# Second attention's scores as twelve 32-row products in row groups instead of four 128-row products

## What is computed

```python
q = proj(hs, Wq, bq, S); k = proj(at, Wk, bk, T); v = proj(at, Wv, bv, T)   # heads of 32 columns
scores = jnp.einsum('bhsd,bhtd->bhst', q, k) / scale
scores = jnp.clip(scores, -50.0, 50.0)
attend = (attention_mask.astype(jnp.float32) > 0.5)[:, None, None, :]
scores = jnp.where(attend, scores, -10000.0)
scores = jnp.clip(scores, -50.0, 50.0)
probs = jax.nn.softmax(scores, axis=-1)
ctx = jnp.einsum('bhst,bhtd->bhsd', probs, v)
```

## Time and profile before

| | us |
|---|---|
| median of 3 runs (2567.28 to 2568.74) | 2568.36 |
| span of the profiled execution | 2568.4 |
| second attention: first clip starts | 1822.25 |
| second attention: last clip ends | 2353.85 |

### The profile page before, as it was taken

The page is one execution under the profiler, slowest core; times in us unless marked ns, Lnnn a source line. Parts: engine busy times, 40 slices in busy tenths (PEclk is TensorE's granted clock), DMA queues, the critical chain, the costliest instruction groups (busy, mean ns, idle before and its releaser), DMA issues. The chain is left out here.

```text
span 2568.4 us, 33913 instructions
## 1 busy us (share of the span) xinstructions
PE 2506.9 (98%) x13273; PEld 1626.8 (63%) x13288; DVE 1786.5 (70%) x2456; ACT 1223.6 (48%) x1853; POOL 1286.9 (50%) x340
## 2 busy tenths in 40 slices
PE   8999999999999999999998999999999999999998
PEld 8988888987545545555544787788533333335786
DVE  4554554556777767777774676664899999999873
ACT  4222313311666666666664232322688888886110
POOL 0000000000999999999993000000599999997310
PEclk9999999999999999999999999999999999999999
DMA  8677776655535345354323754443997777776300
GB/s 303 212 255 236 265 283 240 221 172 160 115 83 121 68 96 108 68 111 93 68 71 137 246 185 156 155 164 87 245 213 168 167 159 167 159 170 196 120 33 33
DMA packets 218865, 405.10 MB, mean 158 GB/s; under 512 B 18217, under 2 KB 94537, under 8 KB 218641
## 3 DMA queue, kind: packets, MB, share of 16 engines
q1 hardware_dynamic: 218704, 402.93, 56.8%
HBM read 260.63 MB, written 140.59 MB: 156 GB/s over the span
## 5 line engine op out<-in xcount | busy, mean ns | idle before, releaser
L1486 POOL TENSOR_TENSOR pooled<-pooled,probs 128x2048 f32<-128x2048 f32 x140 | 641.5, 4582 | 21.0 <-POOL pooled L1486 0.9
L1345 ACT ACTIVATE probs<-psum 128x512 f32<-128x512 f32 (+1 forms) x832 | 449.6, 600 | 333.6 <-PE psum L1231 328.4
L1372 DVE TENSOR_REDUCE win_max<-psum 128x1 f32<-128x802 f32 x480 | 454.3, 988 | 133.9 <-PE psum L1196 133.6
L2271 DVE TENSOR_SCALAR probs<-psum,bound 128x1024 f32<-128x1024 f32 (+1 forms) x416 | 499.0, 1275 | 31.5 <-POOL pooled L2303 21.3
L2246 ACT ACTIVATE probs<-probs 128x1024 f32<-128x1024 f32 (+1 forms) x416 | 437.6, 1059 | 82.5 <-DVE probs L2271 40.6
L2303 POOL TENSOR_TENSOR pooled<-pooled,probs 128x2048 f32<-128x2048 f32 x92 | 424.2, 4611 | 13.2 <-ACT probs L2246 1.0
L1231 PE MATMUL psum<-q_st,k_st 128*128 128x512 f32 (+1 forms) x832 | 318.7, 436 | 22.2 <-ACT probs L1345 15.6
L312 POOL TENSOR_TENSOR r_q<-ve_q,minus_half 128x4 f32<-128x4 f32 x8 | 9.1, 1133 | 611.3 <-DVE ve_q L256 611.3
L1196 PE MATMUL psum<-k_st,q_st 96*128 96x402 f32 x960 | 265.8, 358 | 0.9 <-DVE o_sb L1391 0.4
L1231 PEld LDWEIGHTS psum<-q_st,k_st 128*128 128x128 f32 (+1 forms) x832 | 149.4, 185 | 180.4 <-ACT probs L1345 130.6
L2214 PE MATMUL psum<-q_st,k_st 128*128 128x512 f32 (+1 forms) x832 | 251.6, 428 | 10.7 <-DVE probs L2271 9.6
(11 more groups left out here) (276 smaller groups left out, 4211.1 us busy)
## 6 DMA issues: line engine op xcount, KB each, us to landing
k_st<-k_hi SPq DMA_DIRECT2D x64, 801.0 KB, 10.6
k_st<-k_lo SPq DMA_DIRECT2D x48, 801.0 KB, 11.1
k_hi<-kt_hi SPq DMA_DIRECT2D x32, 801.0 KB
k_lo<-kt_lo SPq DMA_DIRECT2D x32, 801.0 KB
v_rows<-v_out SPq DMA_DIRECT2D x96, 256.0 KB
v_st<-v_rows SPq DMA_DIRECT2D x24, 768.0 KB
q_st<-q_hi SPq DMA_DIRECT2D x64, 256.0 KB, 8.4
w<-w_hi_d SPq DMA_DIRECT2D x64, 256.0 KB, 3.1
```

The source lines that it names most:

```text
L1345: A.activation(probs[i % NPROBS][0:rows, j, :], bank(score_banks.where["score", u, t, j])[0:rows, :], ACT.Exp, scale=1.0 / ROOT).then_inc( ...
L1372: V.tensor_reduce(win_max[:, r, j, c:c + 1], window(windows.where["max", u, i])[:, :, 0:MV], AX.XY, ALU.max).then_inc(max_done, 1)
L1486: G.tensor_tensor(pooled[u % 2][:], before[:], probs[tile(u, k) % NPROBS][:], ALU.add).then_inc(pool_added, 1)
L2271: V.tensor_scalar(probs[i % NPROBS][0:rows, half * W:half * W + W, :], window(("score", u, t, half))[0:rows], bound[0:rows, u // NG, t:t + 1],
```

## The change

Keys and queries keep their natural layout: 128 partitions for the four heads, the high and the low part side by side. A head's product now has 32 rows and lies in the head's own row group of the array (partitions 32j to 32j+31). A tile's scores are three rounds (high by high, high by low, low by high; the low-by-low product is gone), each of four 32-row products, one for each head and row group, into the head's own bank. All twelve follow the waits for both of the tile's windows, and `scored` is signalled in the third round only. Turns give way to steps: one tile's scores, then values and sums of the tile two behind. `last_sum` moves behind the values of tile 1 (step 3), the copy of the sums behind the exponentials of step 3, `copy_acc` behind the first one of step 1. The loads are two a unit for keys and two for queries in place of four and four.

```diff
-            n, NQ, NSLOT = 1, 4, 3
+            n, NQ, NSLOT, LAG = 1, 2, 3, 2
+            TERMS = ((0, 0), (0, 1), (1, 0))
-            PER_TURN, ACC_COPY, DEN_COPY, LAST_SUM = 3, (1, 0), (2, 2), 2
-            VALUES = [[-2], [-1], [0, 1], [2], [3, 4], [5], [6, 7], [8], [9, 10]]
-            TURNS, SUM_LATER = len(VALUES), TT - 3
+            ACC_COPY, DEN_COPY, LAST_SUM, SUM_LATER = (1, 0), (3, 1), 1, TT - 3
...
+                def steps():
                     for u in range(UNITS):
+                        for t in range(TT):
+                            yield u, t, divmod(tile(u, t) - LAG, TT) if tile(u, t) >= LAG else None
...
+                    def scores(u, t):
+                        s, rows = u % NSLOT, TROWS[t]
+                        ps = []
+                        for half in range(HALVES):
+                            pair = take(("score", u, t, half))
+                            windows.freed_by(clipped, score(u, t, half) + 1)
+                            ps += [pair[0:rows, w, :] for w in range(W)]
...
-                        for w in range(W):
-                            m = M.matmul(ps[0:rows, w, :], k_st[s][:, j + w, t * P:t * P + rows],
-                                         q_st[s][:, j + w, :], start=True, stop=True)
-                        m.then_inc(scored, 1)
+                        for i, (of_k, of_q) in enumerate(TERMS):
+                            for j in range(HPG):
+                                head = slice(j * DH, (j + 1) * DH)
+                                m = M.matmul(ps[j], k_st[s][head, of_k, t * P:t * P + rows], q_st[s][head, of_q, :],
+                                             start=i == 0, stop=i == len(TERMS) - 1)
+                                if i == len(TERMS) - 1 and j % W == W - 1:
+                                    m.then_inc(scored, 1)
+
+                    for u, t, behind in steps():
+                        scores(u, t)
+                        if behind:
+                            values(*behind)
+                            if behind != (UNITS - 1, SUM_LATER):
+                                sums(*behind)
+                            if behind[0] and behind[1] == LAST_SUM:
+                                last_sum(behind[0] - 1)
...
                     def load_kq(u):
                         s = u % NSLOT
+                        for h in range(NQ):
                             if u > 1:
+                                load(k_st[s][:, h, :], (k_hi, k_lo)[h][n][u], kq_landed[s])
+                            load(q_st[s][:, h, :], (q_hi, q_lo)[h][n][u], kq_landed[s])
```

More of the change, by code:

```diff
@@ L2048, in sp_program @@
                     Y.wait_ge(hidden_ps, B * FT)
[L2049 to L2054, removed]
+                    for h in range(2):
+                        load(early_k[0][:, h, :], (k_hi, k_lo)[h][1][0], early_landed)
+                        load(x_hi[:, h, :], (q_hi, q_lo)[h][1][0], early_landed)
                     load(v_view[:, 0:TT - 1, :], v_rows[1][0][0:(TT - 1) * P, 0:P].rearrange("(t p) c -> p t c", p=P),
@@ L2062, in sp_program @@
                         if i == 9:
-                            for quarter in range(4):
-                                load(early_k[1][quarter * DH:(quarter + 1) * DH, :, :],
-                                     (k_hi, k_lo)[quarter % 2][1][1].rearrange("(j d) t -> d j t", d=DH), second_landed)
+                            for h in range(2):
+                                load(early_k[1][:, h, :], (k_hi, k_lo)[h][1][1], second_landed)
                 pe_program()
@@ L2073, in ffn_0_and_q_projection_1 @@
                 in_bank = {hidden.where["p", B - 1, g]: (B - 1) * NG + g + 1 for g in range(NG)}
-                return Carried((early_landed, 16 * 10), (second_landed, 16 * 4),
+                return Carried((early_landed, 16 * 6), (second_landed, 16 * 2),
                                [(p_stored[i], 32 * sum(min(place, 2) == i for place in places)) for i in range(3)],
@@ L2146, in inverting @@
                     return u // NG - 1 if u % NG == 1 and u > NG else None
-                def turns():
+                def steps():
                     for u in range(UNITS):
[L2151 to L2154, removed]
+                        for t in range(TT):
+                            yield u, t, divmod(tile(u, t) - LAG, TT) if tile(u, t) >= LAG else None
                 def values(u, t):
@@ L2202, in take @@
                         return psum[:, 2 * slot:2 * slot + 2, :]
[L2204 to L2207, removed]
+                    def scores(u, t):
[5 more added lines that the diff above has]
+                            ps += [pair[0:rows, w, :] for w in range(W)]
+                        if u == t == 0:
                             M.wait_ge(*carried.landed)
-                        elif t == half == 0:
+                        elif t == 0:
                             if u == 1:
@@ L2246, in exps @@
                         A.activation(dst, dst, ACT.Exp, scale=1.0 / ROOT).then_inc(exp_done, 1)
[L2248 to L2251, removed]
+                    for u, t, _ in steps():
+                        for half in range(HALVES):
+                            exps(u, t, half)
+                            if u and (t, half) == ACC_COPY:
                                 copy_acc(u - 1)
-                            if u and (k, i) == DEN_COPY:
+                            if u and (t, half) == DEN_COPY:
                                 copy_den(u - 1)
-                            for g in HIGH_PARTS.get((u, PER_TURN * k + i), ()):
+                            for g in HIGH_PARTS.get((u, t * HALVES + half), ()):
                                 A.wait_ge(last.o_normed, g + 1)
@@ L2278, in dve_program @@
                     V.memset(cols.two[:], 2.0 - 1e-8).then_inc(set_up, 1)
[L2279 to L2282, removed]
+                    for u, t, _ in steps():
+                        for half in range(HALVES):
+                            clip(u, t, half)
+                        if t == 1 and inverting(u) is not None:
                             V.wait_ge(den_landed, 16 * (inverting(u) + 1))
@@ L2334, in load_kq @@
                         s = u % NSLOT
[L2335 to L2338, removed]
+                        for h in range(NQ):
                             if u > 1:
-                                load(k_st[s][rows, :, :], k_src.rearrange("(j d) t -> d j t", d=DH), kq_landed[s])
-                            load(q_st[s][rows, :, :], q_src.rearrange("(j d) t -> d j t", d=DH), kq_landed[s])
+                                load(k_st[s][:, h, :], (k_hi, k_lo)[h][n][u], kq_landed[s])
+                            load(q_st[s][:, h, :], (q_hi, q_lo)[h][n][u], kq_landed[s])
                     def load_v(u):
```

## The result

The changed kernel takes 2595.11 us (median of 4 runs, 2594.87 to 2596.65) against 2568.25 us: a ratio of 1.0105, 95% interval 1.0091 to 1.0119. That is 26.9 us slower, where 20.6 were forecast. The profiled execution's span is 2593.3 us. It stands 24.9 above that of before, less than the medians do, since the profiled execution of before had waited 3.31 us for a transfer at 1387 us, long before the change, which this one had not.

A forecast was written before the change was run, and what follows sets the result against it. POOL's additions bound the kernel at 33.1 us a unit; a DVE-PE ring would make it 34.5 (5 x 2.77 + 3.55 + 7 x 2.44). Units 1 to 14 +19.5, unit 0 -0.1, unit 15 +1.2: +20.6 on 2568.4, 2589 us; range 2565 to 2635.

The forecast's parts named there:

- POOL was the bound: Kernel before: POOL's row of additions sets the pace, 33.1 us a unit, with DVE close behind.
- the ring: DVE's clips and PE's scores wait for each other in turn: 2.44 us a tile where DVE alone needs 2.38.
- PE has slack: Kernel before: a gain on PE alone is worth nothing, a loss costs only beyond 33.1 us a unit.
- Row groups work at once, a round in 0.231: Scores on PE: three rounds of four concurrent 32-row products, 0.69 us a tile against 0.92, worth nothing.
- 0.30 us a round: Rival on PE's scores: slower rounds make the loop 2.58 us and the kernel 2618 us; chance 10%.
- Loads in a row: Rival: PE loads the four row groups' weights one after the other, 0.107 us each; 2700 us; chance 9%.
- products in a row: Rival: PE's products in different row groups run one after the other; about 2950 us; chance 5%.
- Two windows at once take the look-ahead: PE's scores of a tile wait until the first clip of the tile before has ended; this is what costs.
- Steps with sums: Steps where PE also does sums: 2.77 us each, not covered by DVE's loop; five a unit.
- the copy's step: Step 4 of each unit, where sums of tile 2 wait for the copy of the sums: 3.55 us.
- half clock: Unit 0: a stretch at half the clock cost DVE 2.46 us before; half returning gives 34.0 us, so -0.1.
- Loads worth nothing: Transfers of keys and queries: half the bytes and four a unit in place of eight, worth nothing.

The follow-up runs named there:

- split_sums: Changed kernel with the copy of the sums earlier, one window wait a tile, and PE's row sums split into two halves over two steps (tile 2 whole): 2568.76 us.
- old_pool7: Kernel before, with tile 10's addition moved from POOL to PE in every unit: 2567.26 us, ratio 0.9995.
- old_alt: Kernel before, with tile 10's addition moved from POOL to PE in every second unit only: 2562.75 us, ratio 0.9976.
- old_steps_two: Kernel before, with 128-row products, in the order of one tile a step, and both windows of a tile awaited ahead of its first product: 2585.97 us.
- old_steps: Kernel before, with its 128-row products and loads, in the new order of one tile a step; each half waits for its own window alone: 2570.46 us.
- one_wait: Changed kernel, but PE waits only for the later of a tile's two windows: 2586.91 us, ratio to before 1.0075.
- den_early: Changed kernel, with the copy of the row sums moved from behind tile 3's second exponential to behind its first: 2585.25 us, ratio to before 1.0069.
- loads_twice: Changed kernel, with each load of keys and queries made twice, the second into unused space: 2594.97 us, ratio to before 1.0104.
- head_order: Changed kernel, with the loops over rounds and heads exchanged, so a head's three products follow each other: 2599.51 us, a single run.

## Why the prediction was right

The time lies 6 us above the 2589 us forecast and inside its own range (2577 to 2602; 0.05 us in each of 208 steps would be 2579 to 2599). Point by point:

- **POOL was the bound, and the ring takes its place.** Right, by the chain before and after, and by `split_sums`, where POOL comes back. But the step "PE has slack" overstated it: `old_pool7` and `old_alt` put PE at 32.2 of 33.1 us, and the 32.55 us of the earlier trace rows, set aside there as overlapping matmuls, had been near.
- **Row groups work at once, a round in 0.231.** Right: 0.97 us for three rounds, as summed. The second and third round start 0.231 us apart (median of the records). The first two start 0.34 apart, but the first two of four 128-row products are 0.31 apart as well (`old_steps_two`). The 0.30 us a round that the prediction worked out from the 3.07 in the Trainium skill, "TensorE: Matmul & The Clock Gate", Part 3, didn't occur. Loads in a row and products in a row didn't either.
- **Two windows at once take the look-ahead.** Right, shown by `old_steps` against `old_steps_two` (15.5 us). That the rest comes from the late first half is argued, not shown.
- **The ring of 2.44 us.** This is the term that was mis-sized: 2.53 measured. Free window to load was 0.12 and not 0.05, with 0.03 more in the first loads. The forecast took the 0.05 from the kernel before, where a load has one wait; two waits put an instruction of its own between clip and load. `one_wait` gave it back. In a unit this is 7 x 0.09 us more, less what the next point has too much.
- **Steps with sums** 2.73 for 2.77 (2.79 in step 1), **the copy's step** 3.45 for 3.55. `den_early` returned 9.9 us for the 11 worked out. A unit came to 34.8 us for 34.5.
- **Ends.** From the first clip to the last clip's end the stage took 558.1 us against 531.6. The last unit was 35.5 us, as worked out, but by luck: the ring too short and the other steps too long cancel there. The first was 35.0, not 34.0. The measured steps alone, 3 x 2.73 + 10 x 2.53, would make 33.5. The unit's second and third step took 3.22 and 3.35 us in place of 2.53, so the half clock (0.50 granted) cost 1.5 us, where 2.46 would have been all of it and the forecast had taken half. PE had been busy for 0.97 of the 4 us before (columns as in the earlier trace rows):

```profile
1820.00:1824.00 4.00, 0.97 (x12) 0.55 (x12) 4.00 (x7) 2.94 (x4) 0.00 (x0) 0.87 0.49 183
1824.00:1828.00 4.00, 3.95 (x24) 1.61 (x28) 3.26 (x3) 2.90 (x3) 1.74 (x1) 0.50 0.66 192
```

- **Loads worth nothing.** Right, `loads_twice`.

## What to carry to other kernels

A faster way to do a product is paid for by what it must hold at once. As this kernel writes them, four row groups take four banks, two of three windows, and that turned an engine working ahead into a ring in which DVE and PE wait for each other; sum up such a ring from latencies (clip, release, load, rounds, release) and then look at each step that is longer than it, since with nothing in store no such step is made good. Before building, count the nearest engine behind the bound as well: with POOL at 33.1 us a unit and PE at 32.2, an addition moved from one to the other gained nothing in every unit and 6 us in every second, not 12. Whether two heads at a time, in one window, would have kept the look-ahead, no run shows.

## What the runs showed of the hardware

- Four 32-row products with 128 columns of weights and 512 moving columns (float32r tiles), in four row groups and four banks, run at the pace of one 128-row product: 0.231 us from the second round to the third, 0.97 us for three rounds, and 0.57 us for their twelve loads.
- Products in different row groups start out of program order (`head_order`): the product written sixth of twelve starts tenth in 196 of 208 tiles. With the loops exchanged the kernel lost 4 us, in one run, not 200.
- A second wait ahead of a load isn't free, even if it has long been true: 0.07 us more between clip and load, and 0.03 in the first loads, 8.2 us in this kernel (`one_wait`).
